# Splitting the issue of q's transfers: the 8 of the low half from ACT, the 8 of the high half from SP

## The reference, cut to what matters

```python
x = x + tanh(g_xattn[0]) * L0_xattn(layernorm(x), ctx, ...)      # 16 heads of 8, rotary q and k
x = x + tanh(g_ffn[0])   * L0_ffn(layernorm(x), ...)             # 8 experts, top 1, relu
x = x + tanh(g_xattn[1]) * L1_xattn(layernorm(x), ctx, ctx, mask, ...)   # 16 heads of 8, masked
x = x + tanh(g_ffn[1])   * L1_ffn(layernorm(x), ...)             # 8 experts, top 2, silu-gated

q = (xn @ Wq).reshape(b, -1, 16, 8).transpose(0, 2, 1, 3)
attn = softmax(q @ k.T * 8 ** -0.5)                              # k: 77 rows
out = attn @ v
```

## Time and profile before

| | us |
|---|---|
| median of 3 runs | 472.65 |
| lowest and highest | 469.25, 473.23 |
| the profiled execution | 466.07 |
| its span, first to last instruction | 464.2 |

### The profile page before, as it was taken

One profiled execution on the slowest core, in us unless ns is written; L12 is line 12 of the kernel. 1 busy time (PEld: TensorE's weight loads), 2 busy tenths in 40 slices (PEclk: granted clock), 3 DMA queues, 4 the chain that ended last, 5 costly groups with the idle time before them and its releaser, 6 DMA issues.

```text
span 464.2 us, 7008 instructions
## 1 busy us (share of the span) xinstructions
PE 314.7 (68%) x1932; PEld 228.1 (49%) x1932; DVE 264.1 (57%) x916; ACT 136.3 (29%) x302; POOL 152.2 (33%) x172
## 2 busy tenths in 40 slices
PE   2468999989754095751467999999530298888920
PEld 2236555545353094640256566654320297777820
DVE  2768668773675244353367667765545066665634
ACT  2412354535313033220103454354200033333300
POOL 3211212051423134561102102165766134555550
PEclk9767799999985579795567999999855599999985
DMA  7434032100000867823231313000103677988708
GB/s 268 126 74 118 12 80 52 43 11 19 17 8 29 224 215 215 243 73 90 62 85 36 71 27 85 14 24 23 42 29 100 213 244 236 299 249 289 235 12 269
DMA packets 39997, 52.93 MB, mean 114 GB/s; under 512 B 7177, under 2 KB 24334, under 8 KB 39968
## 3 DMA queue, kind: packets, MB, share of 16 engines
q1 hardware_dynamic: 33648, 45.03, 33.7%
q0 software_dynamic: 3584, 6.36, 3.9%
q10 hardware_dynamic: 2736, 1.20, 0.9%
HBM read 35.58 MB, written 9.64 MB: 97 GB/s over the span
## 4 chain that ended last, share of the span: by engine, by line
PE 21%; DVE 8%; issue 7%; DMA 6%; SPq 4%; POOL 4%; ACT 1%; POOLq 0%; DVEq 0%; ACTq 0%
POOL routed L445 3%; PE ps_s L750 2%; PE ps_a L730 2%; DMA xt<-routed 2%; PE ps_a L731 2%; PE ps_s L821 2%; SPq L342 2%; PE ps_s L751 2%; PE ps_t L705 2%; PE ps_n L765 2%; PE ps_a L838 1%; PE ps_d L765 1%; PE ps_t L821 1%; DMA probs<-expert_out 1%; DMA routed<-pay,slot 1%
## 5 line engine op out<-in xcount | busy, mean ns | idle before, releaser
L463 POOL DMA_INDIRECT expert_out<-yo,rows_at x64 | 63.0, 984 | 81.5 <-DVE yo L1179 63.6
L529 ACT ACTIVATE probs<-ps_s 103x512 f32<-103x512 f32 (+1 forms) x96 | 56.3, 597 | 56.8 <-PE ps_s L751 53.3
L445 POOL DMA_INDIRECT routed<-pay,slot x48 | 48.4, 1009 | 58.3 <-DVE slot L1132 47.8
L1025 DVE TENSOR_REDUCE negm<-ps_a 128x4 f32<-128x308 f32 x128 | 55.1, 470 | 19.5 <-PE ps_a L731 18.0
L750 PE MATMUL ps_s<-qs,ks 128*103 128x512 f32 (+1 forms) x96 | 46.2, 481 | 2.0 <-ACT augT L522 1.2
L731 PE MATMUL ps_a<-ks,qs 128*128 128x308 f32 x128 | 43.1, 374 | 5.9 <-DVE negm L1025 5.6
L421 POOL TENSOR_SCALAR ve<-mv 128x4 f32<-128x4 f32 x16 | 4.0, 251 | 116.0 <-DVE mv L975 116.0
L751 PE MATMUL ps_s<-augT,aug 128*103 128x512 f32 (+1 forms) x96 | 39.6, 412 | 0.0
L838 PE MATMUL ps_a<-cst,xt 128*128 128x128 f32 x32 | 11.1, 355 | 39.8 <-DMA xt<-routed 38.2
L731 PEld LDWEIGHTS ps_a<-ks,qs 128*128 128x128 f32 x128 | 28.9, 227 | 15.4 <-DVE negm L1025 6.6
L821 PE MATMUL ps_s<-xT,probs 128*128 128x128 f32 x208 | 32.5, 299 | 2.9 <-DVE xT L1190 1.7
(11 more groups left out here) (168 smaller groups left out, 659.3 us busy)
## 6 DMA issues: line engine op xcount, KB each, us to landing
probs<-f_in SPq DMA_DIRECT2D x40, 384.0 KB
qs<-qhl SPq DMA_DIRECT2D x128, 64.0 KB, 2.0
probs<-f_in SPq DMA_DIRECT2D x24, 321.0 KB
xt<-routed SPq DMA_DIRECT2D x32, 65.0 KB
probs<-routed SPq DMA_DIRECT2D x32, 65.0 KB
yin<-expert_out SPq DMA_DIRECT2D x8, 256.0 KB, 4.4
routed<-pad ACTq DMA_DIRECT2D x18, 65.0 KB
x<-x_in SPq DMA_DIRECT2D x4, 256.0 KB, 7.6
```

The costliest lines, as they stand in the source:

```text
L445: pool.indirect_dma_start(out=routed[l], out_offset=bass.IndirectOffsetOnAxis(ap=slot[c][:, t:t + 1], axis=0), in_=pay[c][:, t, :], in_off ...
L463: pool.indirect_dma_start(out=expert_out[l], out_offset=bass.IndirectOffsetOnAxis(ap=rows_at[i % SHORT][:, :], axis=0), in_=yo[i % SHORT][ ...
L529: nc.scalar.activation(probs[n % 2][0:KSIZE[j], s, :], ps_s[(NS * n + s) % SCORE_BANKS][0:KSIZE[j], :], ACT.Exp, scale=SCALE).then_inc(exp ...
L1025: nc.vector.tensor_reduce(negm[:, i, g * HPG:(g + 1) * HPG], a[:, 0:GK].rearrange("p (h k) -> p h k", h=HPG), AX.X, ALU.max, negate=True). ...
```

## The change

SP issues only the high half's transfers, 8 per block, once the high half is there. ACT gets a new function spread_low, called at the step where the low half is due, after high_q of the same step. It waits for DVE's low half, for n >= 3 also for the scores of block n - 3, and issues the low half's 8 transfers. The transfers themselves and their semaphores are the same.

```diff
@@ spread_q, on SP @@
                 if n >= 3:
                     sp.wait_ge(sc_full, NS * (n - 2))
+                sp.wait_ge(qh_ok, n + 1)
                 for g in range(GROUPS):
-                    for half, ready in enumerate((qh_ok, ql_ok)):
-                        if g == 0:
-                            sp.wait_ge(ready, n + 1)
-                        for c in range(2):
-                            rows = 64 * c + 32 * half
-                            sp.dma_start(qs[n % 3][rows:rows + 32, g, :].bitcast(F32), qhl[half][32 * g:32 * g + 32, :].bitcast(F32)).then_inc(qspread[n % 3][g], 16)
+                    for c in range(2):
+                        sp.dma_start(qs[n % 3][64 * c:64 * c + 32, g, :].bitcast(F32), qhl[0][32 * g:32 * g + 32, :].bitcast(F32)).then_inc(qspread[n % 3][g], 16)
@@ on ACT @@
+            def spread_low(n):
+                act.wait_ge(ql_ok, n + 1)
+                if n >= 3:
+                    act.wait_ge(sc_full, NS * (n - 2))
+                for g in range(GROUPS):
+                    for c in range(2):
+                        act.dma_start(qs[n % 3][64 * c + 32:64 * c + 64, g, :].bitcast(F32), qhl[1][32 * g:32 * g + 32, :].bitcast(F32)).then_inc(qspread[n % 3][g], 16)
+
@@ ACT's steps @@
+                    for b in due("low", k):
+                        spread_low(n0 + b)
                     for b in due("augment", k):
                         copy_augT(n0 + b)
```

## The result

| | kernel before | changed kernel |
|---|---|---|
| median, us | 470.95 (4 runs) | 490.23 (4 runs) |
| lowest and highest, us | 464.37, 473.23 | 487.75, 493.88 |
| ratio of the two, with its 95% interval | | 1.0508 (1.0357 to 1.0659) |
| the profiled execution, us | 466.07 | 491.20 |
| its span, us | 464.2 | 489.4 |

The change makes the kernel slower by 5%. The medians lie 19.3 us apart, the two profiled executions 25.1 us.

The account below looks back on a forecast made before the run. PE was taken to bound the attention, ACT one tile behind. Stalls and gain 17.2, clock 6.8 and slack -1.0 made +23.0 us on the 472.65 us median: 495.6 us, range 483 to 509.

Parts of the forecast that it names:

- The price of an issue on ACT: Per block, ACT's eight low-half issues at SP's pitch of 0.63 us take 5.05 us; lower bound 0.44 us per issue.
- the second rival: ACT issues at 0.44 us: 486 us, chance 0.12; counter-argument: SP's 65 KB issue is also faster, 333 against 591 ns.
- The stops: At n = 2, 3, 6, 7, tile 8's score matmul waits for tile 6's late exponential: +5.0, +3.8, +3.2, +2.5 us.
- n = 0: First block of layer 0: ACT's issues make the first take_keys copy 4.75 us late, costing +4.3 us.
- n = 1: Second block of layer 0: the hold falls where ACT is idle, costing zero; without that cover, 5 us.
- The gain at n = 4: Start of layer 1: block 5's high half starts near 234.0 instead of 235.62, copy_nT now being late next: -1.6 us.
- The clock: Behind the four mid-block stalls, a short half-clock stretch each: 4 x 1.7 = 6.8 us, between 0 and 13.6.
- The slack: PE's existing waits for DVE, such as 1.99 us before 103.24, can shrink: -1.0 us, between 0 and -3.
- The sum: Whole kernel: 17.2 + 6.8 - 1.0 = +23.0 us; profiled execution 489.1 us, median 495.6 us.
- Issues taking turns: SP's and ACT's issues alternate, 8.8 us instead of 5.05 at n = 2: +22 more, 518 us; chance 0.10.
- Cheap issues: ACT issues at 0.44 us, each hold 3.5 us, three clock drops: +13, 486 us; chance 0.12.
- Issues beside ACT's work: ACT computes while issuing, nothing is held, only the start of layer 1 gains 3.1 us: 469.5 us; chance 0.06.

Follow-up runs that it names:

- own buffer: Kernel before with a separate buffer for q's halves of each layer's second block, SP issuing all: 459.9 against 466.6 us, ratio 0.995; again 458.6 against 463.3, 0.997.
- two groups: Kernel before, but ACT issues the low half of groups 0 and 1 only in every block, SP the other 12: 469.0 against 466.6 us, ratio 1.016.
- starts only: Kernel before, but ACT issues the low half for n = 0, 1, 4, 5 only: 471.9 against 466.6 us, ratio 1.025.
- halves swapped: Changed kernel with halves exchanged, ACT issuing the high half and SP the low: 482.8 us against 463.3 of the kernel before, ratio 1.060.
- issued in gaps: Changed kernel's split, but n = 0 issued behind copy_nT of block 1 and n = 2, 3, 6, 7 two transfers per step: 463.6 against 463.3 us before, ratio 1.016.
- middle blocks alone: Kernel before, but ACT issues the low half for n = 2, 3, 6, 7 only: 489.3 against 463.4 us, ratio 1.057.
- the hold without the transfers: Kernel before, SP issuing all 16, plus 8 unread transfers of the same shape issued by ACT in n = 2, 3, 6, 7: 489.9 against 463.4 us, ratio 1.055.
- one pair a step: Kernel before, but in n = 2, 3, 6, 7 ACT issues the low half, one group's two transfers per step: 467.8 against 463.4 us, ratio 1.015.

## Why the prediction was right

**What bounds.** Right: PE in the middle of the attention, ACT one tile behind it. The waits name it: PE for ACT's exponentials 15.2 us after.

**The price of an issue on ACT.** Taken at SP's pitch, 5.05 us for eight; measured 5.02 to 5.29. The bound of 0.44 us per issue, from transfers of another shape, was the wrong row, as the second rival's own counter-argument had it.

**The stops.** Forecast 5.0, 3.8, 3.2 and 2.5 us from the lead of one tile; measured 4.90, 3.93, 3.37 and 2.52. n = 0: forecast 4.3, measured 4.7. n = 1: 0 and 0.1.

**The gain at n = 4.** Forecast -1.6, measured -1.5, and for the reason given: copy_nT is late next. A further 2.3 us came behind it that the sum did not have. Before, PE waited 4.14 us for DVE ahead of block 4's maxima, and the stretch in which they run was mostly at half clock; after, there is no such wait, and they run at full clock. The wait and the stretches of before, then a stretch of the changed kernel:

```profile
237.42 0.63 PE L730 MATMUL ps_a<-aug,maskT 128*128 128x308 f32 x1 [4.14 <-DVE negm L1025]
...
236.00:240.00 4.00, 2.58 (x10) 2.58 (x11) 3.41 (x8) 0.25 (x1) 0.00 (x0) 0.56 0.28 66
240.00:244.00 4.00, 3.71 (x16) 3.46 (x14) 3.79 (x9) 0.00 (x0) 0.00 (x0) 0.59 0.47 110
```

```profile
256.00:260.00 4.00, 4.00 (x21) 3.05 (x22) 4.00 (x11) 0.00 (x0) 0.00 (x0) 1.00 0.81 189
```

So it seems the reverse of a clock drop; the low stretch is missing as well in other kernels with a shorter wait there (own buffer in both profiles, two groups, starts only, halves swapped, issued in gaps), it is there in the one with the middle blocks alone, where the wait is 4.30 us, but also in the one in which only n = 4 and 5 changed. That it is due to the shorter idle time is argued, not shown.

**The clock.** Forecast 6.8 us for four stops. What the four blocks lost beyond their stops is 6.5 - 4.9 = 1.6, 6.8 - 3.9 = 2.9, 5.2 - 3.4 = 1.8 and 4.4 - 2.5 = 1.9, together 8.2. Three stretches were of the short kind and one of the long, where four short ones had been taken. A low stretch behind each stop was not certain, as the stop of 3.22 us without one shows (the hold without the transfers).

**The slack.** Forecast -1.0, since PE's waits for DVE can shrink. Two did: one of 1.09 us (before, 82.85 us) became one of 0.36 us for ACT (after, 100.11 us), and the kernel is 0.75 us less behind after it; in n = 7 one of 0.65 us went, for 0.3 us. That makes -1.05, but the wait that the prediction named, 1.99 us ahead of 103.24, is 1.99 us again, so the size was right by luck. The last row shows what the 2.0 us of "rest of layer 0" in the table mainly are: behind that unchanged wait the low stretch lasts 6.9 us instead of 3.4, and 2.0 us are lost across it.

```profile
82.85 0.66 PE L705 MATMUL ps_t<-cst,pay 128*128 128x128 f32 x4 [1.09 <-DVE pay L980]
...
100.11 0.63 PE L712 MATMUL ps_t<-cst,pay 128*128 128x128 f32 x4 [0.36 <-ACT augT L527]
...
121.80:128.70 6.90, 6.90 (x30) 3.48 (x29) 1.79 (x10) 2.35 (x5) 0.75 (x1) 0.51 0.06 19
```

The sum did not have this. In the experiments' profiles the stretch at this place is 6.9 us long in six, 3.4 in three and missing in three; what decides is not shown.

**The sum.** +23.0 forecast against the profiled execution, +25.1 measured there. That they lie so close is partly luck: the two amounts that the sum did not have, -2.3 at the start of layer 1 and about +2.0 at the end of layer 0's attention, cancel, and what is left is mostly the clock, 8.2 instead of 6.8. For the median, 495.6 were forecast and 490.2 measured. The lower median comes with a median difference of 19.3 us, while the difference of the two profiles is larger: the scatter of the kernel before, some 5%, is as large as the effect, and the 6.6 us between its profile and its median were carried over to a kernel that doesn't show them (491.2 and 490.2).

**The rivals.** Issues taking turns: excluded, both streams keep a pitch of 0.65 us side by side. Cheap issues: excluded by 614 ns. Issues beside ACT's work: excluded as a whole, since PE stops; the overlap that spoke for it exists, an issue runs beside the ACTIVATE ahead of it; but the ACTIVATE behind the issues waits, and that one decides.

## What to carry to other kernels

Before work is moved to the engine with the lowest busy share, look for what stands behind the new instructions in that engine's order and how far ahead of its reader it is; a hold costs what exceeds that lead, in one piece, and may cost a stretch of low clock on top. A queue that nobody waits for is no reason to move its issues: here one instruction in the run waited for a landing, and a second buffer took that wait away without moving work between engines (a gain of 4 us that only the traces show). If issues must go on a compute engine, put one or two behind each of its instructions, where they run beside it, instead of all at once.

## What the runs showed of the hardware that was not expected

DMA issues on ACT run beside the ACTIVATE that precedes them (they start 0.02 us after it does), while one that follows waits for the last of them. The overlap is one-sided (one pair a step, 57.99 and 59.26 us).

Two engines issuing SBUF-to-SBUF transfers of 64 KB at once each keep nearly the pitch of one: 0.65 and 0.66 us against 0.63 of SP alone.

Not every stop of PE brought a stretch of low clock. Of the 15 stops of 2.33 us or more in five of the profiles (change, middle blocks, hold only, two groups, halves swapped), 14 did: either the clock had fallen to 0.50 before the stop was over (the first matmul behind it then takes 0.75 us instead of 0.48), or it fell 0.5 to 1.3 us behind it, and the stretch lasted 3.4 or 6.9 us. Behind one of 3.22 us, and behind those of 2.22 and 1.33 us, none was seen. The same wait of 2.0 us for DVE at the end of layer 0's attention was followed by 3.4 us, by 6.9 us or by none, from kernel to kernel.
